# Adding each state's product by an accumulating DMA issued by POOL instead of a VectorE add

## The chip, the cores and the metric

The kernel runs on one core of one Trainium2 chip. The metric is the device time of one execution in microseconds (us). Three runs of the kernel before gave 3588.16, 3591.86 and 3598.7 us; the median is 3591.86 us.

Engines are named as in the profile: PE is TensorE (PEld its weight loads), DVE is VectorE, ACT is ScalarE, POOL is GpSimd, SP is SyncE, which here only issues DMAs.

## The reference, cut to what matters

The reference is a stack of four small transformer-like layers on an input of 8 batches, 512 positions and 128 channels. The second layer's attention is a pair of selective state-space models (one forward, one on the reversed sequence), and it is the only part that the change touches:

```python
dA = jnp.exp(dt[..., None] * A)
dBx = (dt * xi)[..., None] * Bm[:, :, None, :]

def step(h, inp):
    a, bx, c = inp
    h = a * h + bx
    return (h, jnp.einsum('bds,bs->bd', h, c))
h0 = jnp.zeros((Bb, D_INNER, D_STATE), x.dtype)
_, ys = jax.lax.scan(step, h0, (jnp.moveaxis(dA, 1, 0), jnp.moveaxis(dBx, 1, 0), jnp.moveaxis(Cm, 1, 0)))
y = jnp.moveaxis(ys, 0, 1) + xi * Dp
y = y * jax.nn.silu(z)
return jnp.einsum('ble,de->bld', y, out_proj)
```

There are 256 inner channels (two halves of 128 partitions) and 16 states. For each state `s` the kernel needs a recurrence along the 512 positions, then the product with row `s` of C, and the sum of these 16 products, which starts from `xi * Dp`.

## The kernel before, in words

Everything is stored with the 128 channels on the partitions and the 512 positions along the free dimension; the batches go through the layers one behind the other, several layers at a time. The work is cut into five strands. L does the early feed-forward and attention parts and prepares the later attentions, M projects into and out of the state-space models, S is the states, F the mixture-of-experts feed-forwards, A the softmax attentions. Each engine runs one program, in which the pieces of the strands are interleaved by a table, `ORDER`: the entry `S3F1A2` means three pieces of S, one of F, two of A. Each engine works in the order of its table; an instruction that waits holds everything behind it on its engine. Between engines there are only semaphores.

Strand S runs over 256 states in a row: 8 batches, in each the forward model (`f`) and then the backward one (`b`), in each 16 states; 16 states of one model are called a phase here. For state number `n`:

- SP loads row `s` of B and of C, spread over all partitions, into `bs` and `cs` (three buffers each).
- POOL makes `rb = du * bs`, one instruction for each half of the channels (line 1543; two buffers).
- ACT computes the decay `exp(dt * A)` of one half into the only PSUM bank of the strand (line 1487).
- DVE scans one half (line 1194) from that bank and `rb` into `rh[n % 3]`; then ACT may fill the bank anew for the other half.
- The product with C, in place in `rh`, is made by POOL for even states (two instructions, line 1532) and by DVE for odd ones (one instruction over both halves, line 1200).
- DVE adds `rh` to the sum `xi[p]`, 128 x 1024 floats in one instruction (`add_state`, line 1173), one state later than the scan. The semaphore `s_y` counts the adds. The scan of state `n` waits for the add of state `n - 3`, which frees its `rh` tile, and the multiply of a finished sum by the gate (line 1523, POOL) waits for the last add of its phase.

POOL has more work in the same queue: the expert products of strand F that PE takes as the next matmul's input (lines 1557 and 1563, `tF`), and the copies `strip<-V` for the attentions (line 1576). The expert products wait for loads `cr<-shares` that SP issues.

## Time and profile before

| | before |
|---|---|
| median of 3 runs | 3591.86 us |
| the profiled execution's own time | 3590.76 us |
| its span in the trace | 3589.0 us |
| PE busy | 2713.3 us |
| DVE busy | 2618.9 us |
| ACT busy | 1682.7 us |
| POOL busy | 1696.2 us |
| mean granted clock of TensorE | 0.781 |

The span is what the trace covers, from the first to the last instruction; the execution takes 1.8 us more. Busy times are sums over instructions; a DVE or POOL instruction that starts and then has to wait for the other one is counted as busy for the whole time.

### The profile page before, as it was taken

The numbers are of one execution on the slowest core, as the hardware profiler recorded it, in microseconds if no ns is written. First come the engines' busy times: TensorE is split into PE (matmuls) and PEld (weight loads), VectorE is DVE, ScalarE is ACT, GpSimd is POOL, SyncE is SP. The second block draws the span as 40 slices with busy tenths as digits, with TensorE's granted clock in tenths as the row PEclk, the third lists the DMA queues.
The fourth block names the chain that finished last, engine by engine and source line by source line (L and its number), as shares of the span: only waits on it lengthen the run. The fifth ranks groups of instructions, "written<-read, shape, count | busy, mean of one in ns | idle before, by whom it ended". The sixth has DMA issues, their size and how long they took to land.

```text
span 3589.0 us, 31663 instructions
## 1 busy us (share of the span) xinstructions
PE 2713.3 (76%) x8594; PEld 871.9 (24%) x8594; DVE 2618.9 (73%) x3818; ACT 1682.7 (47%) x2908; POOL 1696.2 (47%) x1349
## 2 busy tenths in 40 slices
PE   5405565888888887788779787888878777987887
PEld 1101122223222222223222222222222222232222
DVE  1687888878898888788878798778868775344351
ACT  3424444563636464364537373555436261532333
POOL 1486676464736465554725464556545551121101
PEclk6656566788879987798879886887679786988768
DMA  1121122131312232222312231223212220111101
GB/s 76 57 88 63 62 96 79 50 102 53 101 46 87 72 107 68 64 82 73 114 41 83 76 103 45 79 81 99 82 61 82 76 92 25 51 56 44 44 26 38
DMA packets 158881, 253.22 MB, mean 71 GB/s; under 512 B 18928, under 2 KB 56688, under 8 KB 158448
## 3 DMA queue, kind: packets, MB, share of 16 engines
q1 hardware_dynamic: 158704, 251.18, 21.8%
q8 instruction: 72, 1.18, 0.1%
q14 instruction: 105, 0.86, 0.1%
HBM read 233.81 MB, written 16.52 MB: 70 GB/s over the span
## 4 chain that ended last, share of the span: by engine, by line
PE 39%; DVE 28%; issue 11%; ACT 9%; DMA 6%; POOL 5%; SPq 3%; DVEq 0%; POOLq 0%; ACTq 0%
PE ps L466 39%; DVE rh L1194 6%; DVE nmx L1115 5%; DMA cr<-shares 4%; DVE xib L1173 3%; ACT ps L1487 2%; DVE xif L1173 2%; SPq L1642 2%; DMA Qs<-cTN 2%; ACT tN L1434 2%; POOL rb L1543 1%; POOL tF L1557 1%; DVE rh L1200 1%; DVE hA L867 1%; ACT L1231 1%
## 5 line engine op out<-in xcount | busy, mean ns | idle before, releaser
L1194 DVE TENSOR_TENSOR_SCAN rh<-ps,rb 128x512 f32<-128x512 f32 x512 | 622.9, 1217 | 105.8 <-ACT ps L1487 102.5
L1115 DVE TENSOR_REDUCE nmx<-ps 128x1 f32<-128x512 f32 (+3 forms) x1024 | 550.2, 583 | 147.9 <-PE ps L466 146.5
L1434 ACT ACTIVATE tN<-ps 128x512 f32<-128x512 f32 (+3 forms) x1024 | 473.8, 515 | 238.2 <-PE ps L466 234.8
L1532 POOL TENSOR_TENSOR rh<-rh,cs 128x512 f32<-128x512 f32 x256 | 391.1, 1532 | 378.4 <-DVE rh L1194 377.8
L466 PE MATMUL ps<-tN,strip 128*64 128x512 f32 (+3 forms) x2048 | 507.6, 574 | 10.1 <-DVE hN L1133 7.2
L466 PE MATMUL ps<-hF,W 128*128 128x512 f32 x592 | 395.4, 755 | 96.3 <-DVE tF L1055 44.4
L1543 POOL TENSOR_TENSOR rb<-duf,bs 128x512 f32<-128x512 f32 x256 | 386.4, 1527 | 115.9 <-DVE rh L1194 110.7
L466 PE MATMUL ps<-tF,W 128*128 128x512 f32 x544 | 353.5, 745 | 89.2 <-POOL tF L1557 71.1
L1543 POOL TENSOR_TENSOR rb<-dub,bs 128x512 f32<-128x512 f32 x256 | 379.1, 1500 | 76.2 <-DVE rh L1194 65.7
L1557 POOL TENSOR_TENSOR tF<-tF,cr 128x512 f32<-128x512 f32 x128 | 172.6, 1348 | 486.7 <-DMA cr<-shares 436.2
L466 PE MATMUL ps<-Ks,Qs 48*128 48x512 bf16 (+3 forms) x1024 | 291.2, 435 | 76.0 <-DVE nmx L1115 69.6
L466 PE MATMUL ps<-Qs,Ks 51*128 51x512 bf16 (+3 forms) x1024 | 231.7, 367 | 106.6 <-ACT tN L1434 52.3
L1487 ACT ACTIVATE ps<-dtb,Am 128x512 f32<-128x512 f32 x256 | 176.8, 691 | 261.5 <-DVE rh L1194 260.0
L1576 POOL COPY strip<-V 128x32 f32<-128x32 f32 x256 | 82.8, 355 | 441.9 <-PE ps L466 439.9
L1487 ACT ACTIVATE ps<-dtf,Am 128x512 f32<-128x512 f32 x256 | 177.1, 692 | 169.4 <-DVE rh L1194 168.9
L1563 POOL TENSOR_TENSOR tF<-hF,cr 128x512 f32<-128x512 f32 x128 | 177.9, 1406 | 124.2 <-DMA cr<-shares 105.0
L1369 ACT ACTIVATE tF<-ps 128x512 f32<-128x512 f32 x144 | 85.8, 596 | 312.8 <-PE ps L466 312.5
L466 PE MATMUL ps<-X,W 128*128 128x512 f32 x192 | 145.0, 855 | 96.1 <-POOL X L1510 39.6
L1173 DVE TENSOR_TENSOR xib<-xib,rh 128x1024 f32<-128x1024 f32 x128 | 198.9, 1554 | 0.3
L1173 DVE TENSOR_TENSOR xif<-xif,rh 128x1024 f32<-128x1024 f32 x128 | 194.3, 1518 | 3.7 <-POOL rh L1532 3.5
L466 PEld LDWEIGHTS ps<-Ks,Qs 48*128 48x128 bf16 x1024 | 64.6, 97 | 530.1 <-DVE nmx L1115 347.6
L466 PEld LDWEIGHTS ps<-Qs,Ks 51*128 51x128 bf16 x1024 | 63.9, 94 | 515.9 <-ACT tN L1434 286.0
(240 smaller groups left out, 3928.0 us busy)
## 6 DMA issues: line engine op xcount, KB each, us to landing
cr<-shares SPq DMA_DIRECT2D x256, 256.0 KB
bs<-rowsf SPq DMA_DIRECT2D x128, 256.0 KB, 3.6
cs<-rowsf SPq DMA_DIRECT2D x128, 256.0 KB, 3.3
bs<-rowsb SPq DMA_DIRECT2D x128, 256.0 KB, 3.7
cs<-rowsb SPq DMA_DIRECT2D x128, 256.0 KB, 3.3
parts<-spl SPq DMA_DIRECT2D x32, 384.0 KB, 2.6
Qs<-parts SPq DMA_DIRECT2D x384, 32.0 KB
Ks<-parts SPq DMA_DIRECT2D x384, 32.0 KB
```

The costliest lines, as they stand in the source:

```text
L466: return eng.matmul(o, l, r, start=start, stop=stop, skip_group_check=skip_group_check)
L1115: red(nmx[:, qt, 8 * a + i:8 * a + i + 1], PA[u % 3][:, 0:nk], AX.X, ALU.max, negate=True).then_inc(s_red, 1)
L1173: tt(xi[p][:, :, :], xi[p][:, :, :], rh[n % NH][:, :, :], ALU.add).then_inc(s_y, 1)
L1194: eng.tensor_tensor_scan(rh[n % NH][:, g, :], PS, rb[n % NBB][:, g, :], 0.0, ALU.mult, ALU.add).then_inc(s_h, 1)
L1369: act(tF[u % NG][:, :], PF[1], ACT.Tanh).then_inc(*F.by_act(j, f"si{u}"))
L1434: act(tN[e % NP][:, q0:T], PA[a][:, 0:T - q0], ACT.Exp).then_inc(s_ex, 1)
L1487: act(PS, dt[p][:, g, :], ACT.Exp, scale=Am[:, at:at + 1]).then_inc(s_a, 1)
L1532: tt(h, h, cs[n % NB][:, :], ALU.mult).then_inc(s_cp, 1)
L1543: tt(rb[n % NBB][:, g, :], du[p][:, g, :], bs[n % NB][:, :], ALU.mult).then_inc(s_bp, 1)
L1557: tt(t, t, cr[n % NC][:, :], ALU.mult).then_inc(*F.by_pool(j, f"w{i}"))
L1563: tt(t, hF[:, :], cr[n % NC][:, :], ALU.mult).then_inc(*F.by_pool(j, f"w{i}"))
L1576: eng.tensor_copy(strips[2 * (p % 2) + a][:, :, 24:32], V9[n % 2][:, :, 8 * a + 4 * g + p, :]).then_inc(s_strip, 1)
```

## The change

DVE's `add_state` is gone. POOL issues a DMA in its place, which reads the 128 x 1024 floats of `rh` and adds them to `xi[p]` in SBUF (`accum_op=ALU.add`). Its end counts 16 on `s_y`, so every threshold on `s_y` is multiplied by 16. POOL issues the DMA of state `n - 2` after the products of state `n`'s turn, and the last three of a phase together; before each one it waits until the DMA of the state before has ended, since all add to the same tile. The ring of `rh` has four tiles instead of three. The tables in `ORDER` are new for all five engines; of these only a line is shown here.

```diff
     "sp": (
-        "M1S17M1S47M1S27F4S4F3S1F1M1F1S14P1S1P2S1P1S3P1S2P1S11M1S13A1S6F6S4F2S2F1S7M1S3P1S2P5S2F4S2F2S2F3S4F1S1F3S1F3A1"
...
+        "M1S18M1S37M1S41M1S7F4S4F2S2F1S2F2S12P4S3P1S2P1M1S9A1S16F1S2F5S3F1S1F2S1M1S6P1S1P4F1P1F3S6F3S2F1S2F1S2F1S2F5S2F"
...
-        NB, NBB, NH = 3, 2, 3
+        NB, NBB, NH = 3, 2, 4
...
             def strand_s():
-                def add_state(n):
-                    k, p, s = SEQ[n]
-                    eng.wait_ge(*times_c_done(n))
-                    if s:
-                        eng.wait_ge(s_y, n)
-                    else:
-                        eng.wait_ge(*jm[k, "m" + p].dve("yi1"))
-                    tt(xi[p][:, :, :], xi[p][:, :, :], rh[n % NH][:, :, :], ALU.add).then_inc(s_y, 1)
-
...
                         if n >= NH:
-                            eng.wait_ge(s_y, n - NH + 1)
+                            eng.wait_ge(s_y, 16 * (n - NH + 1))
...
-                        yield
-                    if s >= 1:
-                        add_state(n - 1)
-                        yield
-                    if s == NS - 1:
-                        add_state(n)
                         yield
...
                         eng.wait_ge(*j.dve("zs1"))
-                        eng.wait_ge(s_y, 32 * b + (16 if p == "f" else 32))
+                        eng.wait_ge(s_y, 16 * (32 * b + (16 if p == "f" else 32)))
...
+
+                def add_state(n):
+                    k, p, s = SEQ[n]
+                    eng.wait_ge(*times_c_done(n))
+                    if n:
+                        eng.wait_ge(s_y, 16 * n)
+                    if s == 0:
+                        eng.wait_ge(*jm[k, "m" + p].dve("yi1"))
+                    eng.dma_start(xi[p][:, :, :], rh[n % NH][:, :, :], accum_op=ALU.add).then_inc(s_y, 16)
...
+                    if s >= 2:
+                        add_state(n - 2)
+                        yield
+                    if s == NS - 1:
+                        for m in (n - 1, n):
+                            add_state(m)
+                            yield
```

What the new tables do on the engines is seen in their instructions. In the following rows the line number stands first, then the instruction with its tiles (with their numbers in their rings), the shape, the semaphores that it waits for, and how many alike follow one another. First DVE in the first phase, where it had scans, products with C and adds in turn. Before:

```order
L986 SCALAR_TENSOR_TENSOR xib<-xib,dub 128x512
L1194 SCALAR_TENSOR_TENSOR rh1<-ps2,rb0 128x512
L1173 TENSOR_TENSOR xif<-xif,rh0 128x1024
L1194 SCALAR_TENSOR_TENSOR rh2<-ps2,rb1 128x512
L986 SCALAR_TENSOR_TENSOR xib<-xib,dub 128x512
L1194 SCALAR_TENSOR_TENSOR rh2<-ps2,rb1 128x512
L1200 TENSOR_TENSOR rh2<-rh2,cs2 128x1024
L1173 TENSOR_TENSOR xif<-xif,rh1 128x1024
L1194 SCALAR_TENSOR_TENSOR rh0<-ps2,rb0 128x512
```

and DVE after the change, some states further on in the same phase:

```order
L1183 SCALAR_TENSOR_TENSOR rh1<-ps2,rb1 128x512 x2
L891 SCALAR_TENSOR_TENSOR tL<-ps0,W,hA 128x512
L1189 TENSOR_TENSOR rh1<-rh1,cs0 128x1024
L1183 SCALAR_TENSOR_TENSOR rh2<-ps2,rb0 128x512 x2
L1183 SCALAR_TENSOR_TENSOR rh3<-ps2,rb1 128x512 x2
L1189 TENSOR_TENSOR rh3<-rh3,cs2 128x1024
```

The instruction of line 1173 is gone after every second scan; scans and products with C are as many as before (line 1194 has become 1183, line 1200 has become 1189).

The second place is the end of a phase on POOL, in the middle of the program, where the backward model's states begin. Before:

```order
L1532 TENSOR_TENSOR rh0<-rh0,cs0 128x512 [waits s_h,s_cs0]
L1576 COPY strip0<-V9_1 128x4x8 [waits s_pv,L_act]
L1576 COPY strip1<-V9_1 128x4x8
L1532 TENSOR_TENSOR rh0<-rh0,cs0 128x512 [waits s_h,s_cs0]
L1576 COPY strip2<-V9_1 128x4x8 [waits s_pv]
L1576 COPY strip3<-V9_1 128x4x8
L1518 TENSOR_TENSOR dub<-dtb,xib 128x1024 [waits M_dve]
L1543 TENSOR_TENSOR rb0<-dub,bs2 128x512 [waits s_h,s_bs2,M_pool] x2
```

and after the change, at the same place:

```order
L1535 TENSOR_TENSOR rb1<-duf,bs1 128x512 [waits s_h,s_bs1] x2
L1556 TENSOR_TENSOR tF2<-tF2,cr0 128x512 [waits F_dve,s_cr0]
L1515 TENSOR_TENSOR rh2<-rh2,cs0 128x512 [waits s_h,s_cs0] x2
L1525 DMA xif<-rh1 128x1024 [waits s_y,s_cv]
L1525 DMA xif<-rh2 128x1024 [waits s_y,s_cp]
L1501 TENSOR_TENSOR dub<-dtb,xib 128x1024 [waits M_dve]
L1525 DMA xif<-rh3 128x1024 [waits s_y,s_cv]
L1535 TENSOR_TENSOR rb0<-dub,bs2 128x512 [waits s_h,s_bs2,M_pool]
L1575 COPY strip0<-V9_1 128x4x8 [waits s_pv,L_act]
```

Three DMAs stand ahead of the next phase's first `rb`, and each of them waits on `s_y` for the one before. Within a phase one DMA stands between the two pairs of `rb` products of successive states. What follows the states in the tables is nearly as long as before: 578 pieces after PE's last piece of M against 572, and 412 after DVE's last piece of S against 410.

## Rows read from the trace of the kernel before

**Rows 1.** The page: busy time of each engine; the granted clock in 40 slices.
```profile
PE 2713.3 (76%) x8594; PEld 871.9 (24%) x8594; DVE 2618.9 (73%) x3818; ACT 1682.7 (47%) x2908; POOL 1696.2 (47%) x1349
...
PEclk6656566788879987798879886887679786988768
```

**Rows 2.** The chain that ended last: by engine (the page), by line (its view).
```profile
PE 39%; DVE 28%; issue 11%; ACT 9%; DMA 6%; POOL 5%; SPq 3%; DVEq 0%; POOLq 0%; ACTq 0%
...
by line: PE ps L466 38.5%; issue 11.4%; DVE rh L1194 6.2%; DVE nmx L1115 5.0%; DMA cr<-shares 3.9%; DVE xib L1173 2.8%; ACT ps L1487 2.1%; DVE xif L1173 2.1%; SPq L1642 1.6%; DMA Qs<-cTN 1.5%; ACT tN L1434 1.5%; POOL rb L1543 1.3%; POOL tF 
```

**Rows 3.** Windows: stretch, length, busy us of each engine, clock, DMA share, GB/s.
```profile
0.00:600.00 600.00, 279.30 (x504) 93.28 (x504) 429.62 (x484) 247.22 (x365) 353.93 (x229) 0.61 0.23 75
600.00:3000.00 2400.00, 1944.34 (x6520) 635.66 (x6520) 1969.37 (x2862) 1223.70 (x2149) 1251.14 (x996) 0.82 0.24 76
3000.00:3589.00 589.00, 489.68 (x1571) 143.00 (x1571) 219.96 (x474) 211.76 (x394) 91.09 (x124) 0.81 0.13 43
1050.00:1200.00 150.00, 127.37 (x390) 37.43 (x388) 130.20 (x164) 90.02 (x157) 87.83 (x70) 0.90 0.27 84
```

**Rows 4.** Groups by line: busy us, mean ns; idle before, and releasers.
```profile
L1194 DVE TENSOR_TENSOR_SCAN rh<-ps,rb 128x512 f32<-128x512 f32 x512 | 622.9, 1217 | 105.8 <-ACT ps L1487 102.5 <-POOL rb L1543 1.8
...
L1532 POOL TENSOR_TENSOR rh<-rh,cs 128x512 f32<-128x512 f32 x256 | 391.1, 1532 | 378.4 <-DVE rh L1194 377.8
L1543 POOL TENSOR_TENSOR rb<-duf,bs 128x512 f32<-128x512 f32 x256 | 386.4, 1527 | 115.9 <-DVE rh L1194 110.7 <-DMA bs<-rowsf 4.7
L1543 POOL TENSOR_TENSOR rb<-dub,bs 128x512 f32<-128x512 f32 x256 | 379.1, 1500 | 76.2 <-DVE rh L1194 65.7 <-DMA bs<-rowsb 5.5 <-issue 4.4
L1173 DVE TENSOR_TENSOR xib<-xib,rh 128x1024 f32<-128x1024 f32 x128 | 198.9, 1554 | 0.3
L1173 DVE TENSOR_TENSOR xif<-xif,rh 128x1024 f32<-128x1024 f32 x128 | 194.3, 1518 | 3.7 <-POOL rh L1532 3.5
L1200 DVE TENSOR_TENSOR rh<-rh,cs 128x1024 f32<-128x1024 f32 x128 | 183.4, 1433 | 7.8
```

**Rows 5.** The adds of line 1173, min/median/max ns; second row between 125 and 250 us.
```profile
L1173 DVE TENSOR_TENSOR xif<-xif,rh x128: 1187/1218/3366, 141.0 to 2781.9; 128x1024 f32<-128x1024 f32 x128
...
L1173 DVE TENSOR_TENSOR xif<-xif,rh x16: 1198/2188/2286, 141.0 to 234.2; 128x1024 f32<-128x1024 f32 x16
```

**Rows 6.** Timeline, 250 to 275 us: start, us, engine, instruction; idle before.
```profile
254.12 6.88 POOL L1543 TENSOR_TENSOR rb<-dub,bs 128x512 f32<-128x512 f32 x4
...
257.60 2.28 DVE L1173 TENSOR_TENSOR xib<-xib,rh 128x1024 f32<-128x1024 f32 x1
257.71 0.32 SPq L1610 DMA_DIRECT2D cs<-rowsb  x1
...
263.01 1.20 DVE L1173 TENSOR_TENSOR xib<-xib,rh 128x1024 f32<-128x1024 f32 x1
...
263.24 2.09 POOL L1532 TENSOR_TENSOR rh<-rh,cs 128x512 f32<-128x512 f32 x1 [0.82 <-DVE rh L1194]
```

**Rows 7.** Groups of POOL between 3000 and 3589 us.
```profile
L1563 POOL TENSOR_TENSOR tF<-hF,cr 128x512 f32<-128x512 f32 x40 | 50.0, 1265 | 105.4 <-DMA cr<-shares 95.2 <-PE ps L466 9.9
```

**Rows 8.** The scans: min/median/max ns, first and last start; who waits for them.
```profile
L1194 DVE TENSOR_TENSOR_SCAN rh<-ps,rb x512: 1184/1217/1225, 130.6 to 2931.1; 128x512 f32<-128x512 f32 x171
```

**Rows 9.** DMA: the main queue's share; issues by line, KB each, us to landing.
```profile
q1 hardware_dynamic: 158704, 251.18, 21.8%
...
bs<-rowsf SPq DMA_DIRECT2D x128, 256.0 KB, 3.6
...
W<-wts SPq DMA_DIRECT2D x1, 1263.0 KB, 7.5
...
W<-wts SPq DMA_DIRECT2D x1, 461.0 KB, 3.7
```

**Rows 10.** The two multiplies of 128 x 1024 on POOL: min/median/max ns.
```profile
L1518 POOL TENSOR_TENSOR duf<-dtf,xif x8: 2342/2352/3256, 123.7 to 2550.0; 128x1024 f32<-128x1024 f32 x8
```

**Rows 11.** The chain between 820 and 870 us, loads of the experts' shares.
```profile
821.39 12.70 DMA cr<-shares
...
836.13 15.50 DMA cr<-shares
```

More of the change, by code:

```diff
@@ new lines @@
+        "1A3M1A1F1A2F1A1F1A3F2A7F1A2F2A4F1A3F2A2F1A1F2A1F1A2F2A1F1A2F2A2F1A2F2A2F1A2F2A1F1A2F2A1F2A3M1F1L1M1L1A1M1L1F1L"
+        "1F1L1F2L2F1M1F2L1A1F1A1L1F2A1L1F1A1M1F1A1L1F2A1L1F2A3F1A1F3A1L1F2A1L1M1F1A1F2A1F1A1L1F2A1F2A1L1F1A1M1F1A1M1F1A"
+        "4F1A1F1A2F1A4F1A1F1A1F6A1L1M1L1M1A1L1A6L1A4L1A2L1A4M1A2L1A6M1A4M1A2L1A10M1A4L1A4M1A8L1A2M1A2L1A2M1A1L1M1L1A1L1"
+        "A3F1A1F1A1M1A1F2A1M1A1L1F1A3F1A1F1A1F1A1L1A2F1A1F1A1L1A1L1A1F1A2F2A1F1A2F1A1F2A1L1A1F2A2F1A1F2A1F1A1F5A1F1A1F2"
+        "A1F1A2F2A2F2A3F1A1L1A2L1A2F1A2M1A2F1A2L1A2L1A2L1A2F2A6M1L1F1A4F1A4F1A2M1A12L1A2M1F1A2F1A2F1A1F1A1F2A1M1L1A1F1A"
@@ L169 @@
+        "A1S4A1S6M1A1S6A1S1F1S1F1S3F1S3F1S3F1L1S2F1S3F1S2M1S3F1S1F3S1F3S1F2S9A1S7A1S3A1S5A1S6A1S4A1S6A1F3S1A1F2S1F1M1F2"
+        "S6M1S13F2S1F1S3F1S2F1S4F1A1S2F1S3F1A1S4A1S8A1S9A1S3A1S4A1S1A1M1S9F1S1F1S2F1M1F1S3F1S2F1S3F1S1F1S12F3S1F3S1F2S1"
+        "1A1S5A1S5A1S4A1S4A1F3A1S1F1A1F1M1A1F11A8F16A3F2A1F1A1F3A1F1A1F1A1F16A9F3A3F3A2F10"
     ),
```

200 lines of the change are left out of this document (95 added, 105 removed).

## The prediction

> **What bounds the kernel now.** I read the page first. PE is busy for 76% of the span, DVE for 73%, POOL and ACT for 47% each [rows 1]: no engine is full, so the time is set by how the queues hand work to each other. The chain that ended last says who holds the others up: PE 39%, DVE 28%, ACT 9%, DMA 6%, POOL 5%, and within DVE's part the adds that the change removes have 2.8% + 2.1% [rows 2]. Then the windows split the run into three stretches [rows 3]. In the first 600 us DVE is busy for 72% of the time, PE for 47%, at a granted clock of 0.61: this is the head, in which states and early layers run before there is enough matmul work. From 600 to 3000 us PE has 81% and DVE 82%, POOL 52%: a joint bound. From 3000 us on the states are done; PE has 83% and DVE 37%. The scans run from 130.6 to 2931.1 us [rows 8], so the change can act only there: 256 states in some 2802 us are 10.9 us for each, 175 us for each of the 16 phases. The last 658 us are untouched but for their order, which is nearly the old one.
>
> The adds themselves: 198.9 + 194.3 = 393.2 us of DVE, 1.536 us each [rows 4]. Their shortest is 1.19 us, yet in the first phase their median is 2.19 us [rows 5]. The timeline shows why. An add that starts while POOL multiplies takes 2.28 us, one that finds POOL idle 1.20 us, and the POOL product that starts just behind that add takes 2.09 us [rows 6]: the two lock each other out for a whole instruction. POOL's products of 128x512 take 1.265 us in the tail, where DVE has no such instructions [rows 7], and 1.50 to 1.53 us over the run [rows 4].
>
> **The change part by part.** The sum is made against the profiled execution, 3590.8 us (span 3589.0 and 1.8 outside it); this lies 1.1 us below the median of 3591.9.
>
> *(a) The adds leave DVE.* All 393 us leave the engine, but only those on the chain shorten it directly: 2.8% + 2.1% of 3589 is 176 us. −176.
>
> *(b) POOL is locked out less.* 768 products of states take 1156.6 us where they would take 768 x 1.265 = 972: 185 us of waiting for DVE's two-operand instructions. The adds are 256 x 1.22 = 312 us of net DVE time, the products with C about half of that (128 x 1.23), and other such instructions I take as equal to those two together; a third to a half of the 185 us comes back, 80 us. POOL is on the chain for 5% of 3589 = 179 us of its 1696 busy, about a tenth, so −8.
>
> *(c) POOL issues 256 DMAs.* No row shows a DMA issued by POOL. Below, the nearest row is SP's issue, 0.32 us [rows 6]; above, POOL's own multiply of the same 128 x 1024 elements, 2.35 us [rows 10]. I take 1.3 us, the middle of the two and about one of POOL's commonest instructions (1.265 us [rows 7]): 333 us of POOL. Between 0 and 3000 us POOL's busy time goes from 1605 to about 1605 − 80 + 333 = 1858, from 53% to 63% at unchanged time; with the queue fuller I put 0.15 of it on the chain instead of a tenth: +50 (12 at 0.32 us, 90 at 2.35 us).
>
> *(d) The accumulates follow one another.* Each waits on POOL for the one before, and behind it in POOL's queue stand the next `rb`, on which DVE's next scan depends, the experts' products for PE, and the copies for the attentions. Its latency has no row. From two loads, 461 KB in 3.7 us and 1263 KB in 7.5 us [rows 9], a transfer costs 1.5 us plus 4.7 us for each 1000 KB. The accumulate moves 512 KB, but must also read what it adds to. Below: 512 KB, 3.9 us; above: two reads and a write one after another, 1536 KB, 8.8 us; I take both reads, 1024 KB, 6.4 us. Within a phase the states come every 10.9 us on average, which hides it; only where they come back to back does it not (two adds in a row start 5.4 us apart, at 257.6 and 263.0 [rows 6]): there 6.4 overruns 5.5. For a third of the 256 states that is 0.9 us each, 77 us of waiting. At the end of each phase three stand in a row, and POOL is held for two latencies, 13 us x 16 = 205 us. Of these 282 us an eighth reaches the chain, between the shares used above: +35 (at 3.9 us 15, at 8.8 us 65).
>
> *(e) The DMA engines get more to do.* The queue moved 251 MB in 21.8% of the 16 engines' time, 321 MB per ms [rows 9]; 1024 KB are 3.3 us of all sixteen, in every 10.9 us. The loads of the experts' shares take 12.7 to 15.5 us and lie on the chain [rows 11], with 3.9% of it [rows 2], 140 us. Sharing the engines for 30% of the time at half speed: 140 x 0.15, rounded: +20 (between 10 and 30).
>
> *(f) The next in line.* Where an add was on the chain, something else was nearly late too. PE is 81% busy in the middle; I let it take back a twelfth of (a), +15 (0 to a third, 60).
>
> *(g) The ring of four tiles.* A scan waits for the accumulate of four states before, where the old one waited for the add of three before. DVE idles for 102.5 us before scans on ACT and 1.8 us on `rb` [rows 4], and no wait for a free tile shows; at 10.9 us for each state an accumulate has over 20 us. Costed at nothing, hidden behind the state period; without that cover it is case (d) again. The tail's order is costed at nothing too, since it is nearly the old one.
>
> Sum: −176 − 8 + 50 + 35 + 20 + 15 = −64 us, so 3590.8 − 64 = **3527 us**, 1.8% faster. With all costs at their low ends: −184 + 12 + 15 + 10 = −147, 3444 us. With all at their high ends: −184 + 90 + 65 + 30 + 60 = +61, 3652 us.
>
> Two rules of the Trainium skill beside this. "DMA: Bandwidth & Descriptors", section "Anatomy of one DMA — SWDGE (gpsimd) path", fits 2.0 us plus the bytes at 436 GB/s to a DMA issued by GpSimd; an estimate from it is 3.2 us for 512 KB. By that figure (d) would be about 13 and the sum 3505 us; no run here shows it yet. "SBUF — State Buffer", section "Who interferes with whom", says that the loser of the shared pair of ports fully blocks, and that an instruction of two SBUF inputs blocks only a GpSimd instruction that reads SBUF. The trace agrees with the first half (2.28 against 1.20 us). The same page's warning that GpSimd cannot write its DMA lists while DVE holds the pair speaks against moving the add to a DMA of POOL.
>
> **The rivals.**
>
> *More than the chain shows (3380 us).* In the best 150 us of the middle PE is granted 0.90, with 85% busy; over the middle 0.82 [rows 3], and in the head's slices 0.5 to 0.6, where PE is often idle [rows 1]. If PE, less held up by DVE, kept 0.90 through the middle, its 1944 us would be 1944 x 0.82 / 0.90 = 1771; 38% of the 173 us, its share of the chain, are 66, on top of cheap issues: 3444 − 66 = 3378. For it: DVE is beside PE the fullest engine, and its queue shortens by 15%. Against it: the chain runs over PE and short hand-overs already.
>
> *No change (3590 us).* PE at 81% and its hand-overs to ACT and DVE's `nmx` take back everything, or the new waits on POOL just eat the gain: (a) and (b) at 184 against costs of 184. For it: the middle's PE share; against it: in the head PE is no bound at all.
>
> *Slower: the accumulates set the pace (3684 us).* One phase needs 16 latencies in series, plus about 13 us until the next phase's first accumulate can be issued (two `rb`, two states of scans and a product with C). A phase has 175 us now, so it decides from (175 − 13) / 16 = 10.1 us for an accumulate, the wait included. At 10.5 us: 130.6 + 16 x 181 + 657 = 3684 us. For it: the loads on the chain [rows 11] take 12.7 to 15.5 us for a tile of half the size; against it: the loads of B's rows, of that size too, land in 3.6 us [rows 9].
>
> *Slower: POOL in the chain (3650 us).* This is the high sum: it takes issues of 2.35 us, 600 us more of POOL, so that POOL in the head has per state 3 x 1.27 + 2.35 = 6.2 us where both engines now need 5.5. The break-even there is 1.7 us for an issue. That the change doesn't do what it says can be left out: the adds are gone from DVE's program.
>
> **How the numbers follow.** The forecast's own case, 3444 to 3575 us, gets 0.45: the signs are sure, the sizes are not. More gain 0.13, no change 0.15, accumulates setting the pace 0.15, POOL's issues 0.12. The range 3430 to 3650 leaves out the large gain and the upper part of the slow cases, 2 in 10. A measurement tells about 0.3% from no change. Faster is 0.45 + 0.13, with 0.01 of the no-change case: 0.59; within 0.3% is the rest of that case, 0.14; slower 0.27.
>
> **What would show it right or wrong.** Line 1173's work gone and DVE near 2220 us busy; POOL's products of states near 1.40 us in the mean; POOL's issue near 1.3 us (wrong above 2, or below 0.6); accumulates that land in about 6.4 us (the forecast falls at 10); POOL waiting for DMA some 280 us in all, most of it at the ends of phases; `cr` loads a little longer; the scans' last start near 2870 instead of 2931 us, and the tail as long as before; PE's clock up in the middle. The prediction is wrong if the scans wait for POOL's `rb` for over 100 us instead of 1.8, or if the last scan starts later than 2931 us.

## The result and the profile after

| | before | after |
|---|---|---|
| median in the same session | 3590.64 us (4 runs, 3588.16 to 3598.7) | **3772.03 us** (4 runs, 3762.38 to 3776.87) |
| ratio, 95% interval | | **1.0501 [1.0476, 1.0526]** |
| span of the profiled execution | 3589.0 us | 3775.1 us |
| first and last scan start | 130.6, 2931.1 us | 132.1, 3098.4 us |
| last scan start to the end of the span | 658 us | 677 us |

The change makes the kernel 5% slower, 122 us above the upper end of the range. The page of the profile after, its busy times, granted clock, DMA queues, chain, and the issues with KB and us to landing:

```profile
PE 2729.0 (72%) x8594; PEld 874.7 (23%) x8594; DVE 2453.3 (65%) x3562; ACT 1644.9 (44%) x2886; POOL 1702.2 (45%) x1605
...
PEclk6655565787876878797888978887868777988768
...
q1 hardware_dynamic: 158704, 251.18, 21.7%
q0 software_dynamic: 36864, 134.23, 18.8%
...
PE 32%; DVE 21%; DMA 16%; issue 14%; POOL 10%; ACT 5%; SPq 2%; POOLq 0%; DVEq 0%; ACTq 0%
PE ps L464 32%; DMA xif<-rh 5%; DMA cr<-shares 5%; DVE nmx L1113 4%; DMA xib<-rh 4%; DVE rh L1183 4%; POOL rb L1535 3%; POOL rh L1515 2%; POOL tF L1556 1%; DMA Qs<-cTN 1%; POOL tF L1562 1%; SPq L1641 1%; DVE rh L1189 1%; ACT tN L1417 1%; ACT ps L1470 1%
...
xif<-rh POOLq DMA_DIRECT2D x128, 512.0 KB, 5.9
xib<-rh POOLq DMA_DIRECT2D x128, 512.0 KB, 6.5
```

Against [rows 1, 2]: the adds are gone from the chain and DVE has 21% of it instead of 28%, but the accumulates stand there with 5% and 4%, and POOL with 10% instead of 5%. Against [rows 9] the same loads take the same share of the DMA engines, and the accumulates come on top with nearly as much. DVE lost 393 us of adds and is only 166 us less busy (2618.9 against 2453.3): something else on DVE grew. The groups by line show it (busy us, mean ns; idle before):

```profile
L1535 POOL TENSOR_TENSOR rb<-duf,bs 128x512 f32<-128x512 f32 x256 | 358.2, 1500 | 30.5 <-DVE rh L1183 21.9 <-DMA bs<-rowsf 8.5
...
L1515 POOL TENSOR_TENSOR rh<-rh,cs 128x512 f32<-128x512 f32 x256 | 346.4, 1393 | 326.5 <-DVE rh L1183 326.2
...
L1556 POOL TENSOR_TENSOR tF<-tF,cr 128x512 f32<-128x512 f32 x128 | 165.6, 1294 | 597.2 <-DMA cr<-shares 520.5 <-DVE tF L1058 61.4 <-DVE tF L1053 15.2
L1525 POOL DMA_DIRECT2D xif<-rh x128 | 114.3, 893 | 184.3 <-DMA xif<-rh 170.0 <-issue 6.5 <-DVE rh L1183 5.1
L1525 POOL DMA_DIRECT2D xib<-rh x128 | 113.3, 885 | 127.1 <-DMA xib<-rh 106.8 <-issue 7.6 <-DVE rh L1183 5.6
...
L1183 DVE TENSOR_TENSOR_SCAN rh<-ps,rb 128x512 f32<-128x512 f32 x512 | 623.3, 1217 | 248.9 <-ACT ps L1470 153.4 <-POOL rb L1535 81.7 <-DMA xif<-rh 7.4
...
L1189 DVE TENSOR_TENSOR rh<-rh,cs 128x1024 f32<-128x1024 f32 x128 | 232.1, 1813 | 24.2 <-DMA cs<-rowsb 13.1 <-DMA cs<-rowsf 4.0 <-issue 0.3
```

An issue takes 0.89 us, POOL waits 277 us for accumulates, and the scans idle 249 us instead of 106, 82 of it for `rb`. And DVE's product with C, untouched by the change, takes 1813 ns in the mean instead of 1433 [rows 4]. The timeline of one of them in the second phase (start, us, engine, instruction; idle before):

```profile
388.97 2.75 POOL L1535 TENSOR_TENSOR rb<-duf,bs 128x512 f32<-128x512 f32 x2
...
390.82 5.33 DVE L1189 TENSOR_TENSOR rh<-rh,cs 128x1024 f32<-128x1024 f32 x1
...
391.39 1.16 POOL L1525 DMA_DIRECT2D xif<-rh  x1
392.00 3.06 POOL L1535 TENSOR_TENSOR rb<-duf,bs 128x512 f32<-128x512 f32 x2
...
396.08 1.21 DVE L1183 TENSOR_TENSOR_SCAN rh<-ps,rb 128x512 f32<-128x512 f32 x1
```

The product starts at 390.82 us, while POOL works, and ends at 396.15 us; at its own 1.2 us it can have run only after POOL's train had ended at 395.06. In the kernel before, DVE was shut out for one POOL instruction and came in between two [rows 6]. Here it was shut out for a product, an issue and two products. POOL's instructions also overlap: the DMA starts 0.33 us before the pair of 388.97 has ended, the next pair 0.55 us before the DMA has.

I counted this over all instructions of both traces. Call POOL instructions that follow one another without a pause a train. In the kernel before, the next instruction of a train starts 0.04 us before the end of the one ahead of it. In the kernel after, that is so as long as no DMA issue has come in the train; behind an issue, up to eight instructions later, it is 0.31 us in the mean. DVE instructions that take over 0.3 us more than the shortest of their form: before, 281 of them lie across one POOL instruction and one across two; after, 109 across one and 86 across two to eight, all 86 in trains with an issue (how an overlap at an edge is counted moves some ten cases from one side to the other). What DVE's instructions take over their shortest sums to 328 us before (89 of it in the adds) and 438 us after (none in adds).

### The profile page after: what moved, and what is told of

It reads as the page before. It is cut to its first block, busy times and chain, and to the rows that moved or that the text cites. A ratio compares the mean times of both kernels' runs of the same rounds, so it can differ in the third digit from the quotient of the medians.

```text
span 3775.1 us, 31643 instructions
## 1 busy us (share of the span) xinstructions
PE 2729.0 (72%) x8594; PEld 874.7 (23%) x8594; DVE 2453.3 (65%) x3562; ACT 1644.9 (44%) x2886; POOL 1702.2 (45%) x1605
## 3 DMA queue, kind: packets, MB, share of 16 engines
q1 hardware_dynamic: 158704, 251.18, 21.7%
q0 software_dynamic: 36864, 134.23, 18.8%
## 4 chain that ended last, share of the span: by engine, by line
PE 32%; DVE 21%; DMA 16%; issue 14%; POOL 10%; ACT 5%; SPq 2%; POOLq 0%; DVEq 0%; ACTq 0%
PE ps L464 32%; DMA xif<-rh 5%; DMA cr<-shares 5%; DVE nmx L1113 4%; DMA xib<-rh 4%; DVE rh L1183 4%; POOL rb L1535 3%; POOL rh L1515 2%; POOL tF L1556 1%; DMA Qs<-cTN 1%; POOL tF L1562 1%; SPq L1641 1%; DVE rh L1189 1%; ACT tN L1417 1%; ACT ps L1470 1%
## 5 line engine op out<-in xcount | busy, mean ns | idle before, releaser
L464 PE MATMUL ps<-tN,strip 128*64 128x512 f32 (+3 forms) x2048 | 522.6, 590 | 8.1 <-DVE hN L1131 8.1
L1515 POOL TENSOR_TENSOR rh<-rh,cs 128x512 f32<-128x512 f32 x256 | 346.4, 1393 | 326.5 <-DVE rh L1183 326.2
L1535 POOL TENSOR_TENSOR rb<-dub,bs 128x512 f32<-128x512 f32 x256 | 355.3, 1499 | 40.3 <-DMA bs<-rowsb 33.7
L1535 POOL TENSOR_TENSOR rb<-duf,bs 128x512 f32<-128x512 f32 x256 | 358.2, 1500 | 30.5 <-DVE rh L1183 21.9
L464 PE MATMUL ps<-Qs,Ks 51*128 51x512 bf16 (+3 forms) x1024 | 240.5, 375 | 121.3 <-ACT tN L1417 65.5
L1575 POOL COPY strip<-V 128x32 f32<-128x32 f32 x256 | 69.5, 340 | 423.8 <-PE ps L464 414.7
L1189 DVE TENSOR_TENSOR rh<-rh,cs 128x1024 f32<-128x1024 f32 x128 | 232.1, 1813 | 24.2 <-DMA cs<-rowsb 13.1
L1562 POOL TENSOR_TENSOR tF<-hF,cr 128x512 f32<-128x512 f32 x128 | 166.6, 1331 | 154.4 <-DMA cr<-shares 125.7
L1525 POOL DMA_DIRECT2D xif<-rh x128 | 114.3, 893 | 184.3 <-DMA xif<-rh 170.0
L464 PEld LDWEIGHTS ps<-tF,W 128*128 128x128 f32 x544 | 111.0, 228 | 296.8 <-POOL tF L1556 154.8
```

The lines of the kernel that those rows point to most:

```text
L464: return eng.matmul(o, l, r, start=start, stop=stop, skip_group_check=skip_group_check)
L1189: tt(rh[n % NH][:, :, :], rh[n % NH][:, :, :], cs[n % NB][:, :].unsqueeze(1).broadcast_to([128, 2, T]), ALU.mult).then_inc(s_cv, 1)
L1515: tt(h, h, cs[n % NB][:, :], ALU.mult).then_inc(s_cp, 1)
L1525: eng.dma_start(xi[p][:, :, :], rh[n % NH][:, :, :], accum_op=ALU.add).then_inc(s_y, 16)
L1535: tt(rb[n % NBB][:, g, :], du[p][:, g, :], bs[n % NB][:, :], ALU.mult).then_inc(s_bp, 1)
L1562: tt(t, hF[:, :], cr[n % NC][:, :], ALU.mult).then_inc(*F.by_pool(j, f"w{i}"))
```

## The theories

- **L, the lockout.** Behind a DMA issue, POOL's next instructions run into each other, and DVE's instructions, mostly those of two operands, are kept out for the whole train.
- **W, the waits.** The accumulates follow one another, and POOL is held for each landing, with `rb` and the experts' products behind it. This is the prediction's term (d).
- **C, the traffic.** 134 MB more on the DMA engines delay other loads. This is term (e).
- **T, the tables.** The new order itself costs time. The prediction had nothing for it (g).

The runs were made in several sessions beside the kernel before, whose median went from 3586.9 to 3593.0 us. So runs are compared by their ratio to it, and a difference of ratios is turned into us with 3590 us; by the intervals such a difference is known to some 10 us.

## Experiments

**e1: the adds nearly gone from the kernel before.** Of each add only 8 of 512 columns are done, so the sum is incomplete.

```diff
-                    tt(xi[p][:, :, :], xi[p][:, :, :], rh[n % NH][:, :, :], ALU.add).then_inc(s_y, 1)
+                    tt(xi[p][:, :, 0:8], xi[p][:, :, 0:8], rh[n % NH][:, :, 0:8], ALU.add).then_inc(s_y, 1)
```

> The kernel before, tables and all, but DVE adds only 8 of the 512 columns of each half's product to the sum (the output lacks the rest), so each add costs about 0.1 us instead of 1.54. It asks what taking the adds off DVE is worth by itself. The prediction's terms (a) and (b) expect about 3590 - 176 - 8 + 10 = 3415 us, DVE busy near 2260. A theory in which PE and its hand-overs take everything back expects 3560 or more.

Measured: 3492.71 us, ratio 0.9741 [0.9726, 0.9756], last scan start 2832.4 us. The work of the adds is worth 93 us, half of what (a) and (b) put on it. The small adds still take 128 us of DVE (523 and 475 ns where the median is 168): part of an add's price is the wait for POOL, which a short one pays too.

**e2: the new tables and ring, with DVE's adds and no DMA.** Each add stands one state behind its scan.

```diff
-                    eng.dma_start(xi[p][:, :, :], rh[n % NH][:, :, :], accum_op=ALU.add).then_inc(s_y, 16)
+                    tt(xi[p][:, :, :], xi[p][:, :, :], rh[n % NH][:, :, :], ALU.add).then_inc(s_y, 1)
```

> The changed kernel's tables for all engines and its ring of four tiles, but the adds are DVE's again, each one state after its scan as before, and POOL issues no DMA. If the new tables by themselves cost the time, this is near 3770 us. If the DMAs do (their waits on POOL, or DVE being locked out), this is within 2% of the kernel before, 3590 to 3660 us, DVE busy near 2620.

Measured: 3687.04 us, ratio 1.0281 [1.0261, 1.0302]. With full adds the new tables cost 101 us.

**e6: the same with adds of 8 columns** (the sum is incomplete), to see the tables without the adds for which they leave no room.

> The tables and the ring of the change, no DMA at all, and DVE adds one state after the scan, of 8 of the 512 columns (so the sum is left incomplete). Beside it stand 3492.7 us for the same cut with the tables of before, and 3687.0 us for these tables with full adds. If the new tables cost the same with any adds (T), about 100 us: 3590 (3570 to 3610). If their cost in the run with full adds came from adds standing where these tables leave no room for them (the tables are written for a DVE without adds), the small ones are nearly free: 3500 (3480 to 3530), and the tables are not a cause of the loss in the changed kernel.

Measured: 3522.41 us, ratio 0.9805 [0.9787, 0.9822]. Beside e1 the new tables, with the fourth `rh` tile, cost 23 us, not 101: the rest of e2's loss comes only with full adds, in an order not made for them. Of the 23, some 16 lie behind the states: from the last scan's start to the end of the span there are 675 us here (3527.7 − 2852.8) and 659 in e1 (3491.1 − 2832.4).

**e3: the change with accumulates of 8 columns** (the sum is incomplete); issues, waits and tables stay.

```diff
-                    eng.dma_start(xi[p][:, :, :], rh[n % NH][:, :, :], accum_op=ALU.add).then_inc(s_y, 16)
+                    eng.dma_start(xi[p][:, :, 0:8], rh[n % NH][:, :, 0:8], accum_op=ALU.add).then_inc(s_y, 16)
```

> The changed kernel, but each accumulating DMA moves 8 columns of each half instead of 512 (the sum lacks the rest). Issues on POOL and their order stay, landing gets short and the DMA engines free. Theory W (accumulates in series hold POOL: 277 us of waits for landings): POOL's waits for them fall below 60 us, time below 3600 us. Theory L (DVE is locked out by POOL for several instructions in a row behind a DMA issue, 198 us more on DVE's two-operand instructions): DVE busy stays near 2450 us and the time above 3680 us.

Measured: 3696.02 us, ratio 1.0304 [1.0289, 1.0319]. The accumulates land in 4.0 us instead of 6, the DMA engines are nearly free of them, and only 71 us come back. So W and C together are not the whole loss. The long lockouts are all there: DVE's product with C takes 2022 ns in the mean. They are even heavier: the issue of 8 columns holds POOL for 1.24 us instead of 0.89, the overlaps behind it are 0.45 us instead of 0.31, and what DVE's instructions take over their shortest is some 480 us instead of 438. So full transfers probably cost more than these 71 us.

**e4: the change, with POOL waiting until the issue itself is done** before its next instruction. It doesn't wait for the landing.

```diff
-                    eng.dma_start(xi[p][:, :, :], rh[n % NH][:, :, :], accum_op=ALU.add).then_inc(s_y, 16)
+                    eng.dma_start(xi[p][:, :, :], rh[n % NH][:, :, :], accum_op=ALU.add, engine_sem=s_gen).then_inc(s_y, 16)
+                    eng.wait_ge(s_gen, n + 1)
```

> The changed kernel, but behind each DMA issue POOL waits until the issue itself is finished on POOL (a semaphore that POOL counts up at the end of the issue) before its next instruction. Theory L: if the lock is passed from instruction to instruction because the next one starts before the issue has ended, DVE's long waits (over one POOL instruction, about 90 of them) go away, DVE busy falls from 2453 to below 2350 and the time by 50 to 150 us. Theory W: DVE may change, the time does not, or grows by the extra waits, 3770 to 3800 us.

Measured: 3638.58 us, ratio 1.0137 [1.012, 1.0154], 131 us better than the change by adding a wait. Groups by line of e4:

```profile
L1537 POOL TENSOR_TENSOR rb<-duf,bs 128x512 f32<-128x512 f32 x256 | 345.6, 1364 | 34.4 <-DVE rh L1184 20.7 <-issue 5.8
...
L1526 POOL DMA_DIRECT2D xif<-rh x128 | 111.0, 867 | 185.8 <-DMA xif<-rh 160.2 <-DVE rh L1184 16.4 <-issue 7.4
L1526 POOL DMA_DIRECT2D xib<-rh x128 | 110.7, 865 | 147.9 <-DMA xib<-rh 112.3 <-DVE rh L1184 14.2 <-PE ps L465 9.7
...
L1184 DVE TENSOR_TENSOR_SCAN rh<-ps,rb 128x512 f32<-128x512 f32 x512 | 623.7, 1218 | 314.5 <-POOL rb L1537 149.2 <-ACT ps L1471 131.3 <-DMA xib<-rh 18.9
...
L1190 DVE TENSOR_TENSOR rh<-rh,cs 128x1024 f32<-128x1024 f32 x128 | 177.2, 1384 | 25.6 <-DMA cs<-rowsb 13.7 <-DMA cs<-rowsf 4.3 <-DVE rh L1184 0.5
```

and its timeline in the second phase:

```profile
372.69 0.88 POOL L1526 DMA_DIRECT2D xif<-rh  x1
...
373.65 2.48 POOL L1537 TENSOR_TENSOR rb<-duf,bs 128x512 f32<-128x512 f32 x2
...
375.26 1.96 DVE L1190 TENSOR_TENSOR rh<-rh,cs 128x1024 f32<-128x1024 f32 x1
...
376.10 3.31 POOL L1507 TENSOR_TENSOR xib<-xib,dtb 128x1024 f32<-128x1024 f32 x1
```

The product with C is back to 1384 ns; where it starts in the middle of a pair (375.26) it comes in behind it, and POOL's next one waits (3.31 us instead of 2.33). Two products of POOL take 2.48 us together, after the change 2.75 or more. Lockouts over two or more POOL instructions fell from 86 to 2, and DVE's excess from 438 to 224 us. POOL waits for accumulates as long as before (272 us), so nothing of the gain is W's. L is shown as far as the wait goes: the lockouts go, and 131 us with them, when POOL waits for the end of its issue. Why the instructions run into each other, no run shows. The Trainium skill has a sentence that would fit ("GPSIMD Engine Reference", section "Instruction dispatch"): successive Pool instructions are no barrier between the engine's cores, each core goes on to the next one as soon as its share is done. An issue that keeps some cores longer than others would then leave them spread out over the next instructions; the overlaps of 0.31 us, and of 0.45 us in e3 behind the longer issue, agree with it, and the cause stays argued. The rule that the prediction took from the Trainium skill's page "SBUF — State Buffer" (section "Who interferes with whom"), that the loser is blocked for the whole of one instruction, holds in the kernel before (281 of 282 cases) and not behind an issue here (5.33 us for a product of 1.2).

**e5: e4 with accumulates of 8 columns** (the sum is incomplete): W and C once more, now without the lockouts.

> The kernel in which POOL waits after each DMA until its issue is done (3638.6 us), with the accumulates cut from 512 to 8 columns of each half (so the sum is left incomplete). It leaves the port waits as they are there and takes away most of the landing time and of the traffic. If the serial accumulates hold POOL on the path (W), this gives back what the same cut gave without the issue wait, 76 us: 3563 (3545 to 3585). If the wait for the accumulates mostly lay beside the lockouts (L), and the two losses overlap, it gives under 35 us: 3605 to 3640. If only the new tables remain (T), the end is near the run with new tables and small DVE adds, within 20 us of it.

Measured: 3505.89 us, ratio 0.9755 [0.974, 0.9771]. Full transfers cost 137 us here, more than either theory expected, and 71 us while the lockouts were there (e3). Beside small transfers the lockouts cost 197 us (e3 against e5), beside full ones 131. The two losses may overlap, but the lockouts of e3 are also the heavier ones; the runs don't part these two reasons. The small transfers are a control with a flaw: their issues take 1.19 us instead of 0.87, which is 82 us more of POOL, so the cost of full transfers is read too low rather than too high. And 256 issues with their waits cost no more than what they replace: e5 is 18 us faster than e6, in which small adds stand in DVE's queue in their place.

**e9: e4 with each tile added to itself.** The sum of the states is left out; size, kind, number and place of the transfers stay, and none waits for the one before. This parts W from C.

```diff
-                    if n:
-                        eng.wait_ge(s_y, 16 * n)
...
-                    eng.dma_start(xi[p][:, :, :], rh[n % NH][:, :, :], accum_op=ALU.add, engine_sem=s_gen).then_inc(s_y, 16)
+                    eng.dma_start(rh[n % NH][:, :, :], rh[n % NH][:, :, :], accum_op=ALU.add,
+                                  engine_sem=s_gen).then_inc(s_ys[n % NH], 16)
```

> The kernel with the wait for the issue (3638.6 us), in which each of the 256 DMAs adds its rh tile to itself instead of to xi (so the sum of the states is left out): the same 512 KB, the same kind of transfer, the same places, but none waits for the one before. Cutting the transfers to 8 columns gave 133 us. If it was the wait for the one before that costs (W), most of that comes back with the full bytes too: 3530 (3505 to 3560), with the landing still near 6 us. If it was the traffic, which slows the loads of bs, cs and cr (3.4 to 6 us of landing), the time stays: 3620 (3595 to 3640).

Measured: 3611.29 us, ratio 1.0053 [1.003, 1.0077]. Without any wait for the one before, 30 of the 137 us come back; 107 stay, and they are the traffic's. So W is worth 30 us, C 107, each within 10 us. Groups of e9:

```profile
L1527 POOL DMA_DIRECT2D rh<-rh x256 | 220.6, 862 | 8.1 <-DVE rh L1192 5.5 <-DMA rh<-rh 1.5 <-issue 0.3
L1566 POOL TENSOR_TENSOR tF<-hF,cr 128x512 f32<-128x512 f32 x128 | 168.8, 1334 | 163.7 <-DMA cr<-shares 133.5 <-PE ps L467 27.5 <-DMA rh<-rh 1.7
L1560 POOL TENSOR_TENSOR tF<-tF,cr 128x512 f32<-128x512 f32 x128 | 164.1, 1282 | 625.5 <-DMA cr<-shares 539.8 <-DVE tF L1061 68.1 <-issue 17.3
```

and of e5, the same groups:

```profile
L1558 POOL TENSOR_TENSOR tF<-tF,cr 128x512 f32<-128x512 f32 x128 | 165.7, 1294 | 535.3 <-DMA cr<-shares 425.9 <-DVE tF L1059 79.4 <-DVE tF L1054 15.1
L1564 POOL TENSOR_TENSOR tF<-hF,cr 128x512 f32<-128x512 f32 x128 | 165.3, 1306 | 127.4 <-DMA cr<-shares 96.7 <-PE ps L465 29.4
```

POOL's waits for the loads of `cr` grew from 523 to 673 us, PE's waits for POOL's `tF` from 90 to 164, and the loads of B's rows land in 5.5 and 6.3 us instead of 3.6 and 3.7. PE and DVE are as busy as in e5 and POOL less: the transfers keep no engine longer at its work, they delay loads. Which ones, four more runs tell.

**e13 and e14: e9 and e5 with small loads of `bs` and `cs`** (the states use old rows of B and C).

```diff
-                    dma(bs[n % NB][:, :], rows[p][s:s + 1, :].broadcast_to([128, T])).then_inc(s_bs[n % NB], 16)
+                    w = T if n < NB else 8
+                    dma(bs[n % NB][:, 0:w], rows[p][s:s + 1, 0:w].broadcast_to([128, w])).then_inc(s_bs[n % NB], 16)
```

> The run with each tile added to itself (3611.3 us; full transfers, none waiting for the one before), in which SP's loads of rows of B and C fill only 8 of the 512 columns after the first three (so the states use old rows: bs and cs are wrong). It takes away those loads as something that the transfers can delay, and 67 MB of reads. If the 105 us of the transfers come from bs and cs landing late (5.5 to 6.3 us instead of 3.6), nearly all of it goes: 3515 (3490 to 3540), and the pair with small transfers gains under 20 us by the same cut. If they come by the loads of cr and the other loads, 3590 (3570 to 3610), some 20 us for the queues being emptier.

> The run with the wait for the issue and accumulates of 8 columns (3505.9 us) with the same cut of the loads of bs and cs. The control for the other: what the cut gives where nothing delays the loads. They waited 40 us for rb's bs and DVE's cs together there, of which a third is on the path: 3490 (3475 to 3503).

Measured: 3554.73 us, ratio 0.9901 [0.9872, 0.993], and 3460.74 us, ratio 0.9643 [0.962, 0.9666]. The traffic still costs 93 of 107 us. My first guess, that B's rows land late, was wrong. Nor is it the sum of the bytes: e13 loads 131 MB less than e9 (120.61 instead of 251.18 MB on that queue), about what the accumulates add, and keeps nearly the whole cost.

**e15 and e16: e9 and e5 with small loads of `cr`** (the experts are weighted by old values), by the same edit at that load; `bs` and `cs` are whole again.

> The run with each tile added to itself (3611.3 us), its loads of bs and cs whole again, and SP's loads of cr (the experts' gate rows, for POOL's products that PE takes next) filling 8 of 512 columns after the first three (so the experts are weighted by old values). In the pairs of traces POOL's waits for cr grew by 150 us with the full transfers and PE's waits for POOL's tF by 73. If the transfers' 105 us come by these loads, the pair of this cut differs by 0 to 40 us, this one at 3450 to 3500. If they come by all loads alike, it differs by 70 to 90, and this one stands at 3530 to 3560.

> The run with the wait for the issue and accumulates of 8 columns (3505.9 us) with the same cut of the loads of cr, as the control of the other: POOL waits 523 us for cr there, most of it at places where PE works on other strands. 3455 (3430 to 3480).

Measured: 3315.05 us, ratio 0.9235 [0.9208, 0.9262], and 3287.71 us, ratio 0.9169 [0.9137, 0.92]. Now the traffic costs 24 us: most of the 107 came by the loads of `cr`. Their part may be somewhat less than the difference of 83 us, since the cut also shortens the waits for these loads themselves (POOL's from 673 to 333 us in e9, from 523 to 287 in e5), and what is delayed elsewhere can hide behind other work then. Both runs were much faster than I expected. The loads of `cr`, with their 67 MB, hold 210 us of e5 and 294 us of e9.

**e11: e4 with a ring of three `rh` tiles**, the fourth tile by itself.

> The kernel with the wait for the issue and a ring of three tiles: nothing else changed. The prediction costed the fourth tile at nothing. With an accumulate issued two states late that takes 6 us, the scan of state n waits for one issued only some 3 to 5 us before rb of its own is ready. If the ring matters: 3700 (3665 to 3740). If not, because the scans wait for POOL's rb behind the same DMA anyway: 3645 (3635 to 3660).

Measured: 3712.09 us, ratio 1.034 [1.0312, 1.0368], 73 us slower than e4. The scans wait 187 us for accumulates (97.7 + 89.3) instead of 19 or less for each. An add by DMA holds its tile longer, and the fourth tile pays for that.

**e7: e4 with the accumulates of a phase's end spread**, each two states behind its scan or just ahead of the multiply by the gate.

> The kernel with the wait for the issue (3638.6 us), in which the last accumulates of a phase no longer stand together: each stands two states after its scan throughout, also across the phase ends, or just ahead of the gate's multiply. If the 160 us that POOL waits for accumulates at L1525 and its twin, three quarters of them at phase ends, hold the next phase's rb on the path (W), a third to a half comes back: 3590 (3570 to 3615). If they lie beside other work (L), or the wait moves to the multiply by the gate, which needs the last one anyway: 3630 to 3645. POOL's waits for DMA at the accumulates should fall from 272 us to under 120 either way.

Measured: 3737.14 us, ratio 1.0397 [1.037, 1.0423], 93 us slower than e4, outside what either theory had. POOL's waits for accumulates fell only from 272 to 252 us. By state they were never mostly at the phase ends: in e4 the last two states of the 16 phases hold 99 of 333 us of idle before an issue, and the even states within the phases nearly all the rest, since an even state's issue stands only two `rb` behind the odd one's. The multiply by the gate shows what was lost. In e4, at the end of the first phase:

```profile
261.21 2.48 POOL L1537 TENSOR_TENSOR rb<-dub,bs 128x512 f32<-128x512 f32 x2
263.65 3.32 POOL L1507 TENSOR_TENSOR xif<-xif,dtf 128x1024 f32<-128x1024 f32 x1
```

and in e7:

```profile
265.61 0.88 POOL L1549 DMA_DIRECT2D xib<-rh  x1 [4.53 <-DVE rh L1191]
...
279.37 0.88 POOL L1549 DMA_DIRECT2D xib<-rh  x1 [4.44 <-DMA xib<-rh]
280.34 2.33 POOL L1514 TENSOR_TENSOR xif<-xif,dtf 128x1024 f32<-128x1024 f32 x1
```

The finished sum comes 17 us later, behind the next phase's work, which waits for scans and for loads of its own; the last such multiply of `xif` is 95 us late (2924 against 2829 us), and PE waits 117 us for these 16 multiplies instead of 58. Bunching the last three was the better order. That the late multiplies are the whole 93 us isn't shown.

**e10: e4 with two sums.** Odd states go to `xi`, even ones to a second tile in place of the fourth of the ring; POOL adds the two ahead of the gate. It computes everything.

```diff
-                    if n:
-                        eng.wait_ge(s_y, 16 * n)
+                    sem_d, count = added(n)
+                    if count > 16:
+                        eng.wait_ge(sem_d, count - 16)
...
+                    eng.dma_start((acc if SUM[n] else xi[p])[:, :, :], rh[n % NH][:, :, :],
+                                  **({"accum_op": ALU.add} if old else {}), engine_sem=s_gen).then_inc(sem_d, 16)
```

> The kernel with the wait for the issue, complete, with two sums: odd states go to xi, even ones to a second tile of the same size, which takes the place of the fourth tile of the ring; POOL adds the two just ahead of the multiply by the gate (16 instructions of 2.4 us, 39 us of POOL). Neighbouring accumulates no longer wait for each other. W: of 133 us most comes back, less some 5 to 10 for POOL's adds and what the ring of three costs: 3575 (3550 to 3605). Traffic: 3645 (3630 to 3665). If the ring of three costs over 40 us, the run with that alone shows it.

Measured: 3702.4 us, ratio 1.0303 [1.0276, 1.033]. POOL idles 23 us ahead of its issues instead of 312 in e11, and the time falls by 13 us beside e11, which the two intervals hardly tell from nothing. W's 30 us (e9) less POOL's 16 adds would fit it; the ring of three costs the rest. In the room there is, curing the waits costs a tile that is worth more. (In nine of the 16 phases state 0 still goes to `xi`, in one of them state 2 too.)

**e8 and e12: the kernel before with a part of the adds by DMA.** Its own tables and ring of three; the products of states 0, 2, ..., 12 of a phase go into a second tile by POOL's DMA with the wait for the issue, DVE adds nine and the second tile. In e12 the six accumulates of a phase have 8 columns (the sum is incomplete).

```diff
+        D_POOL = [s % 2 == 0 and s <= 12 for s in range(NS)]
...
-                    if s >= 1:
+                    if s >= 1 and not D_POOL[s - 1]:
                         add_state(n - 1)
...
+                            eng.dma_start(acc[:, :, :], rh[n % NH][:, :, :],
+                                          **({"accum_op": ALU.add} if n % NS else {}), engine_sem=s_gen).then_inc(s_d, 16)
+                            eng.wait_ge(s_gen, gone)
```

> The kernel before with its own tables and its ring of three; the products of states 0, 2, ..., 12 of each phase go into a second accumulator by POOL's DMA (a copy, then six accumulates, each with the wait for its issue, issued right behind POOL's own product with C), DVE adds the other nine and the second accumulator: 10 adds a phase instead of 16. All adds made nearly free were worth 94 us in these tables; six of sixteen are worth 35 of them. Against it stand 112 issues of 0.9 us and their waits (1.3 us each as POOL sees them, 145 us of POOL), on the path by the 10 per cent that POOL has of the chain: 15 us; and the wait of scan n for an accumulate that has landed, 6 us after the issue, where the ring of three is one tile short: 0 to 60 us. With W that last cost decides: 3600 (3570 to 3640). If POOL's accumulates are harmless once the issue is waited for (L alone was the loss): 3567 (3550 to 3580).

> The mixed kernel in the tables of before (3606.6 us; seven states of each phase go by DMA into a second sum, DVE adds the other nine), its six accumulates a phase cut from 512 to 8 columns (so the sum is left incomplete; the copy of state 0 stays whole). 50 of 59 MB of transfers go away, issues, waits for issues and places stay. If a MB costs what it did with the new tables (105 us for 134 MB, from the run with each tile added to itself), the traffic is the loss here too: 3606 less 39, 3568 (3555 to 3580), which is the gain that six adds fewer promised. If the issues or the moved places cost, and the traffic is harmless in these tables: 3600 (3590 to 3612).

Measured: 3606.55 us, ratio 1.0039 [1.0027, 1.0052] for e8, and 3580.64 us, ratio 0.9971 [0.9958, 0.9985] for e12. In the tables of before 50 MB of traffic cost 24 us, 0.5 us a MB where the new tables had 0.8 (107 for 134). Without traffic the six adds fewer bring 10 us, not the 35 that e1's 93 promised in proportion. So also here the transfers turn a small gain into a small loss. What eats the other 25 us is open.

**e17: the kernel before with five `cr` tiles instead of three.**

> The kernel before, complete, with a ring of five cr tiles instead of three (4 KB more a partition, as much as the fourth rh tile of the change takes); nothing else changed. POOL waits 541 us for the loads of cr there, PE 238 us for POOL's tF, and the loads made small took over 200 us off the changed kernels. If the loads stand behind a free tile of the ring, two more tiles start them earlier: 3540 (3500 to 3570), and the cost of traffic on them could be hidden. If they stand behind SP's order or behind shares, that is, the first of each eight is late and the rest follow at the pace of the queue: 3588 (3578 to 3598).

Measured: 3595.8 us, ratio 1.0016 [1.0003, 1.0028]: within 0.3%. A free tile is not what these loads wait for.

Not run: the tables of before with all adds by DMA. In each placement that I worked out POOL and DVE would wait for each other; no run shows it. So the tables' part is known with small adds and with full ones, not with the DMA. No version that computes everything beat the kernel before.

## Why the prediction was wrong

The 180 us (0.0501 x 3590), step by step from the kernel before. Each row is a step from the row above, and is known to some 10 us; in another order of the steps the sizes would differ (the lockouts are 131 or 197 us):

| step | runs | us |
|---|---|---|
| DVE's adds nearly gone | e1 | −93 |
| new tables, ring of four | e6 against e1 | +23 |
| small DMAs with the wait for the issue in place of small adds | e5 against e6 | −18 |
| full transfers: traffic | e9 against e5 | +107 |
| full transfers: waits for the one before | e4 against e9 | +30 |
| no wait for the issue: lockouts | after against e4 | +131 |

- **(a), with (f), −161: too large.** All the work of the adds was worth 93 us, with the relief of POOL in it. The chain's shares, 2.8% + 2.1%, named the right instructions, but only about half of the time came back. The prediction gave a twelfth of it to what stood next in line; what holds the rest was not tested.
- **(b) −8: half of the mechanism.** The prediction had seen DVE and POOL lock each other out [rows 6] and reckoned only with less of it. For POOL that came about: by busy time its 768 products take 358.2 + 355.3 + 346.4 = 1060 us instead of 1157, 97 us less where 80 were expected, 1.38 us each where 1.40 was. (Their mean durations, 1.50 us for `rb`, count the overlaps twice.) **The step that failed first is in (b) and (c) together:** (b) counted the lockouts only as something that shrinks, and (c) priced the moved add only as time on POOL's queue. What the issue does to the lockouts behind it, on DVE's side, was left at nothing, and it cost 131 us. DVE, expected near 2220 us busy, stood at 2453 us, and at 2242 in e4, where POOL waits for the issue.
- **(c) +50: no run shows such a cost of POOL's time.** An issue takes 0.89 us instead of 1.3, and e5 is 18 us faster with 256 of them, each of 1.19 us and waited for, than e6 with small adds on DVE. What the small adds themselves cost isn't measured, so the price of the issues alone stays open. The warning that an issue suffers while DVE holds the ports did not show: in e4 none for `xif` took over 1.01 us. (1858 us of 3000 are 62%, not 63; it changes nothing.)
- **(d) +35: right, by luck in its parts.** Landing 5.9 and 6.5 us (6.4 taken), POOL waiting 277 us (282 reckoned), 30 us on the path. (The high end, 65 at 8.8 us, comes out as 70 by the prediction's own steps: 282 + 282 us, an eighth of it.) But the waits lie mostly within the phases and not at their ends; e7, built on that belief, lost 93 us. The estimate from the Trainium skill, 3.2 us ("DMA: Bandwidth & Descriptors", section "Anatomy of one DMA — SWDGE (gpsimd) path"), was half the landing measured; even 8 KB by the same path landed in 4.0.
- **(e) +20: mis-sized five times, 107.** The place was right: the loads of `cr`, on which most of it hangs (e15, e16). The share of the chain was the wrong measure: 3.9% are 140 us, but e5 is 210 us faster with these loads cut, and while POOL's waits for them grew by 150 us, some 107 − 24 = 83 us reached the end. POOL waited 541 us for them already in the kernel before (its groups have 436.2 and 105.0), which the prediction did not count.
- **(g) 0: right on the tile, wrong on the order.** The scans wait only 12 us for a free one of the four tiles (7.4 + 4.7), and without the fourth the kernel is 73 us slower (e11). The tables' own order cost 23 us, 16 of it in the tail, which the prediction took as unchanged.
- **The sum.** Forecast −64, measured +180: the 244 us between them are 131 of lockouts, 87 of (e), 76 of (a), (b) and (f) together (93 gained instead of 169), and 23 of (g), less 68 of (c) and 5 of (d).
- **The rivals.** Landing stayed far below 10.1 us and the issue below 1.7, so neither slower case came by its own mechanism. Of the two signs named at the end one fired: the last scan starts at 3098 us, later than 2931. The other did not: `rb` is waited for 82 us, below the 100 that were named, and still a large part of the scans' new idle time. It was no good sign: in e4, 131 us faster, the scans wait 149 us for `rb`.

In the middle stretch, from 600 to 3100 us (length, busy us of each engine, clock, DMA share, GB/s), the kernel after has:

```profile
600.00:3100.00 2500.00, 1931.94 (x6388) 631.66 (x6388) 1808.14 (x2635) 1194.86 (x2123) 1284.26 (x1196) 0.81 0.46 115
```

Against [rows 3] PE is down from 81% to 77% busy, DVE from 82% to 72%, POOL stands at 51% after 52%, the DMA engines up from 0.24 to 0.46. All engines are emptier and the time longer. The granted clock is 0.81 against 0.82, and PE is busy for 1932 us against 1944 in the 2400 us of before, so PE's own pace explains nothing of it. PE's clock did not go up; the prediction had expected it to.

## What to carry to other kernels

Before work moves from one engine to another's queue, ask what it does to the instructions behind it there: here the DMA issue took 0.9 us, and the train of POOL instructions behind it kept DVE out for up to eight instructions until a wait on the issue's own completion parted them. Before bytes are added to the DMA engines, look for loads that an engine already waits for by the hundred us; here their share of the chain (3.9%, 140 us) understated what they hold (210 us), and cutting their size in a test kernel measured it. And price the removal of work from the path by a kernel without it: the chain's share gave nearly twice what it was worth (176 and 93 us).

## What the runs showed of the hardware

- Behind a DMA issue POOL's back-to-back instructions overlap by 0.31 us instead of 0.04 (0.45 in e3, behind issues of 1.24 us), and DVE's instructions, mostly those of two operands, are shut out for whole trains (5.33 us for one of 1.2 us). A wait on the issue's completion ends both (e4: overlaps of 0.04 us again), for 131 us in 256 issues.
- An accumulating SBUF-to-SBUF DMA of 512 KB issued by POOL holds POOL for 0.87 to 0.89 us and lands in 5.9 to 6.5 us (medians of the kernel after and e4); one of 8 KB for 1.2 us, landing in 4.0 (e3, e5). 256 of the large ones take 18.8% of the 16 engines, as 251 MB of loads take 21.7%.
- With that traffic, loads of 256 KB on SP's queue land later (e9 against e5): those of B's rows in 5.5 and 6.3 us instead of 3.6 and 3.7, those of C's rows in 4.6 instead of 3.4.
